# All 64 second-layer scatters in one row in the attention stage, two in flight

## What is computed

```
xn = layernorm(x)
x  = x + attention(xn) + moe(xn)
```

```
h = rmsnorm(xn) * norm_w                    # 2048 x 256
top 4 of 32 experts by softmax(h @ gate_w.T), weights renormalised
pos = rank of a token within its expert; those past the capacity are dropped
buf[expert, pos] = h[token]                 # the scatter
eo = (silu(buf @ w13_gate) * (buf @ w13_up)) @ w2
out[token] += weight * eo[expert, pos]
```

## Time and profile before

| what | value |
|---|---|
| median of three runs | 1323.95 us |
| the profiled execution, its own time | 1324.33 us |
| its span | 1323.1 us |
| TensorE busy | 1102.8 us (83%) |
| DVE busy | 780.4 us (59%) |
| ACT busy | 522.8 us (40%) |
| POOL busy | 510.3 us (39%), 487 instructions |
| mean granted TensorE clock | 0.921 |
| second route stage | from 890.9 us to the barrier ahead of 957.06 us |
| attention stage | from 957.06 us to the barrier ahead of 1069.65 us |

### The profile page before, as it was taken

One profiled execution on the slowest core, in us unless ns is written; L12 is line 12 of the kernel. 1 busy time (PEld: TensorE's weight loads), 2 busy tenths in 40 slices (PEclk: granted clock), 3 DMA queues, 4 the chain that ended last, 5 costly groups with the idle time before them and its releaser, 6 DMA issues. The chain is left out here.

```text
span 1323.1 us, 19843 instructions
## 1 busy us (share of the span) xinstructions
PE 1102.8 (83%) x5538; PEld 827.4 (63%) x5538; DVE 780.4 (59%) x1925; ACT 522.8 (40%) x1419; POOL 510.3 (39%) x487
## 2 busy tenths in 40 slices
PE   5659999999969999688889999959679979999100
PEld 5436667777859998355557777855357658888100
DVE  5868776666115554599997776257337545545233
ACT  2336765555204444355555555031123324444000
POOL 0657776565000000565565564033634300000575
PEclk9879999999979999699999999979969979999655
DMA  9432222221455654422222221035579235554343
GB/s 359 186 100 84 89 93 80 76 72 53 191 143 175 182 180 156 109 75 76 77 72 72 77 72 32 1 84 230 184 223 273 101 93 163 162 162 156 99 130 112
DMA packets 116998, 167.21 MB, mean 126 GB/s; under 512 B 15248, under 2 KB 88848, under 8 KB 114832
## 3 DMA queue, kind: packets, MB, share of 16 engines
q1 hardware_dynamic: 77248, 107.46, 26.3%
q0 software_dynamic: 12288, 33.57, 8.0%
q10 hardware_dynamic: 27360, 24.92, 5.4%
HBM read 103.11 MB, written 62.78 MB: 125 GB/s over the span
## 5 line engine op out<-in xcount | busy, mean ns | idle before, releaser
L1219 PE MATMUL bank<-big_a,probsT 128*128 x760 | 201.8, 361 | 0.1
L856 POOL TENSOR_TENSOR parts<-wq,parts 128x256 fp32r<-128x256 f32 x64 | 48.9, 764 | 382.6 <-ACT parts L1101 382.6
L1110 ACT ACTIVATE probs<-bank,negmax 128x256 f32<-128x256 f32 (+3 forms) x256 | 135.0, 537 | 121.4 <-DVE negmax L1025 112.8
L917 PE MATMUL bank<-kT,qT 128*128 128x256 f32 (+3 forms) x512 | 171.7, 457 | 0.0
L933 PE MATMUL bank<-const,probs 128*128 128x128 f32 x640 | 129.6, 275 | 26.8 <-DVE probs L1037 26.7
L949 PE MATMUL bank<-probsT,big_b 128*128 128x512 f32 (+3 forms) x512 | 149.1, 434 | 0.0
L1219 PEld LDWEIGHTS bank<-big_a,probsT 128*128 128x128 f32 x760 | 131.6, 196 | 20.8 <-issue 2.2
L1025 DVE TENSOR_REDUCE negmax<-bank 128x1 f32<-128x256 f32 (+3 forms) x256 | 113.6, 486 | 47.4 <-PE bank L919 46.2
L1297 DVE TENSOR_TENSOR work<-work,bank 128x96 f32<-128x96 f32 (+1 forms) x190 | 51.6, 271 | 151.5 <-ACT work L1264 151.4
L1708 POOL DMA_INDIRECT big_a<-ys_dram,slot_r x64 | 62.4, 975 | 200.2 <-PEq L1691 181.0
L901 PE MATMUL bank<-parts 128*128 128x512 f32 x256 | 116.9, 492 | 20.3 <-POOL parts L856 15.3
(11 more groups left out here) (210 smaller groups left out, 2023.3 us busy)
## 6 DMA issues: line engine op xcount, KB each, us to landing
probs<-xs_dram SPq DMA_DIRECT2D x190, 128.0 KB
ys_dram<-work ACTq DMA_DIRECT2D x190, 128.0 KB
work<-khT_dram SPq DMA_DIRECT2D x64, 256.0 KB
xs_dram<-big_a SPq DMA_DIRECT2D x12, 1024.0 KB, 20.0
wq<-in_wq SPq DMA_DIRECT2D x64, 128.0 KB
big_a<-in_gu SPq DMA_DIRECT2D x1, 6144.0 KB, 18.2
stack_dram<-parts SPq DMA_DIRECT2D x24, 256.0 KB
xlow<-stack_dram SPq DMA_DIRECT2D x48, 128.0 KB
```

Of the source, the lines that this page charges most:

```text
L917: nc.tensor.matmul(s.ps[bank][:, at:at + w], s.qT[:, par, i * P:(i + 1) * P], s.kT[:, par, 0:w], start=True, stop=False)
L1110: nc.scalar.activation(s.probs[:, par, ROW_AT[i]:ROW_AT[i] + (i + 1) * P], s.ps[bank][:, at:at + (i + 1) * P], ACT.Exp, bias=s.negmax[:, p ...
L1219: mm = nc.tensor.matmul(s.ps[2 + i % 2][:, 0:W], rowsT[:, i % 2, k * P:(k + 1) * P], gu[:, k, bass.ds(e * W, W)], start=k == 0, stop=k == ...
```

## The change

The 24 scatters of the second route stage are taken out of it, with the wait for the slots and the wait for their landing. All 64 scatters are issued by POOL in the attention stage, in one row, tile by tile and choice by choice. They wait no longer for `shift_ready` of any unit. In front of scatter n (from the third on) POOL waits until scatter n - 2 has landed. At the end it waits for all 64.

```
--- before.py
+++ after.py
@@ -34,7 +34,6 @@
 USED_TILES = (TOKENS * TOPK + EXPERTS * (P - 1)) // P
 UNROLL = 4
 STEPS = 8
-EARLY_TILES = 6
 CAP1 = 2 * TOKENS * TOPK // EXPERTS
 OUT_OF_RANGE = 1 << 16
 
@@ -472,13 +471,8 @@
                     nc.gpsimd.tensor_tensor(k_lo, k_full, k_hi.bitcast(F32), ALU.subtract).then_inc(low_ready, 1)
 
                 split_low(0)
-                pool.wait_ge(slots_done, 1)
                 for b in range(1, BATCH):
-                    for t in (2 * b - 2, 2 * b - 1):
-                        scatter_tile(nc, s, d, 1, t, moved)
                     split_low(b)
-                for k in range(TOPK):
-                    pool.wait_ge(moved[k], 16 * EARLY_TILES)
 
         @block.scalar
         def _(act):
@@ -1512,13 +1506,14 @@
 
         @block.gpsimd
         def _(pool):
-            late = [(t, k) for t in range(EARLY_TILES, TILES) for k in range(TOPK)]
-            for u in range(NU):
-                pool.wait_ge(shift_ready, u + 1)
-                for t, k in late[len(late) * u // NU:len(late) * (u + 1) // NU]:
+            for t in range(TILES):
+                for k in range(TOPK):
+                    n = t * TOPK + k - 2
+                    if n >= 0:
+                        pool.wait_ge(moved[n % TOPK], 16 * (n // TOPK + 1))
                     scatter_tile(nc, s, d, 1, t, moved, (k,))
             for k in range(TOPK):
-                pool.wait_ge(moved[k], 16 * (TILES - EARLY_TILES))
+                pool.wait_ge(moved[k], 16 * TILES)
 
         @block.tensor
         def _(pe):
```

## The result

| | before | changed |
|---|---|---|
| median of 4 runs each | 1323.53 us | 1345.60 us |
| ratio | | 1.0167 (95% interval 1.0149 to 1.0185) |
| the profiled execution, its own time | 1324.33 us | 1344.64 us |
| its span | 1323.1 us | 1342.9 us |

The change costs 22 us. That it would cost time was forecast, how much was not: 1331.5 us was forecast, 7.6 us more than before, and 1345.6 lies outside the range of 1318.3 to 1341.

The account below looks back on a forecast made before the run. POOL's scatters were taken to bound the route stage's end, TensorE the attention stage. With the new row ending after TensorE, the expert stage starts 7.6 us later: 1324.33 + 7.6 = 1331.9, median 0.38 lower, 1331.5 us; range 1318.3 to 1341.

Parts of the forecast that it names:

- The route stage (6.1 us earlier): End of second route stage: without 24 scatters POOL's low parts end sooner, stage ends 6.1 us earlier, bounds 5.5 and 6.7.
- The first loads (1.0 us): Attention stage's start: some 5 scatters beside SP's first loads delay TensorE by 1.0 us, bounds 0 and 1.8.
- The stage ends with the last landing, and SP starts 0.82 us later: Attention stage's end: last scatter lands at 1076.5, SP starts the expert stage 0.82 us after, at 1077.3.
- nothing else of POOL is queued behind the waits: Attention stage's end: POOL has no further work of its own after its waits; no time was added for any.
- The row's length: Attention stage: 64 scatters paced by landing plus restart over two, last landing 12.8 us after TensorE's part ends.
- The free spacing (1.59): Row on nearly free DMA engines: (2.4 landing + 0.78 restart) / 2 = 1.59 us per scatter.
- the full stretch: Row from 966 to 1004 us, DMA engines loaded: landing 4.5 us, spacing 2.64, 14.4 scatters.
- the half-full stretch: Row from 1004 to 1024 us, DMA share 0.78: landing 3.4 us, spacing 2.1, 9.5 scatters.
- 5 to 7 us: Landing times read from two loaded scatters in the earlier trace, behind others in flight and expert weights.
- The clock (0, bound +4): Expert stage's start: TensorE, idle longer before it, may start at the lower clock; taken as 0, bounds 0 and +4 us.
- The first (the row is hidden): Attention stage: landings stay near 2.4 us, row lands at 1054, TensorE's end decides, 1318.9 us; chance 0.22.
- the third rival: Attention stage: SP's queue starves the row, landings 6.0 and 4.5 us, row 17 us late, 1341 us; chance 0.12.

Follow-up runs that it names:

- experiments 1 and 2: 1: changed kernel without the wait on scatter n - 2, 1317.03 us; 2: changed route stage, four attention-stage scatters behind each unit's shift_ready, 1320.15 us.
- experiment 3: Changed kernel, but SP loads the attention stage's expert weights only after all 64 scatters landed: 1327.61 us, with a shorter layer 0 in it.
- experiment 4: Changed kernel, but each scatter waits for the one just before it, one in flight: 1413.58 us, with a shorter layer 0 in it.

## Why the prediction was right and wrong

**The route stage (6.1 us earlier): right.** Measured 6.6 us. The mechanism holds, POOL's scatters between ACT and the last low part, and experiments 1 and 2 get the same 59.6 to 59.7 us.

**The first loads (1.0 us): too much, within its bounds.** TensorE's first matmul (timeline of PE) comes 9.5 us after SP's first load at 952.37, against 9.4 before, although four scatters start beside the loads:

```profile
961.89 0.80 PE L1536 MATMUL bank<-xlow 96*128 96x512 f32 x1 [11.48 <-DMA probs<-in_sums]
```

DVE ends at 1063.98, or 1062.1 without the 1.9 us ahead of the stages; 1063.7 was forecast.

**"The stage ends with the last landing, and SP starts 0.82 us later": this step failed.** The prediction took the 0.82 us from DVE's end and gave it to POOL's. Behind POOL's last landing come a DRAIN of 5.28 us and the barrier, 6.3 us. Half of the attention stage's miss is this term, and by itself it is more than the 4.6 us by which the time lies above the range. It stood in the trace of before, as a DRAIN of 3316 ns, hidden; "nothing else of POOL is queued behind the waits" was wrong.

**The row's length: the mechanism right, the term under-sized by 5.4 us.** The free spacing (1.59) is as measured. In the full stretch the landing was taken as 4.5 us and is 4.2 in the median; 15 scatters start there and 14.4 were forecast. The misses are beside it: 4 and not 5.4 in the first loads, 8 and not 9.5 in the half-full stretch, where the landing is 4.1 in the median and not 3.4. With 30 scatters by then in place of 32.5, 2.5 more go at 1.59 each, 4 us; the rest is a few single late steps, such as 1.56 us of idle time at 1042.78 among those of 0.92. That the landing in the full stretch came out as forecast is in part luck: "5 to 7 us" reads too much into the earlier trace rows, where the scatter of 978.84 has its packets between 983 and 985, which is 4 to 6 us.

**The clock (0, bound +4): about right.** The expert stage takes 164.5 in place of 163.6 us. The granted clock is 0.59 in 1090 to 1100 and 1.00 from 1100 on (changed, the last two rows); in the same first 10 us of the stage it was 0.70 before (first row):

```profile
1070.00:1080.00 10.00, 8.31 (x34) 6.11 (x35) 3.11 (x10) 2.37 (x6) 0.00 (x0) 0.70 0.40 118
...
1090.00:1100.00 10.00, 8.25 (x29) 6.06 (x30) 2.92 (x10) 2.05 (x5) 0.00 (x0) 0.59 0.34 105
1100.00:1200.00 100.00, 100.00 (x556) 84.48 (x555) 50.15 (x184) 40.50 (x124) 0.00 (x0) 1.00 0.52 163
```

So the stage began in part at the lower level before as well. The difference of 0.9 us is within the bounds; that it is the clock's was not tested.

**The rivals.** The first (the row is hidden) falls with its constant landing: the landings go with the load, 4.2 us in the median of one stretch and 2.4 in another. The Trainium skill, DMA: Bandwidth & Descriptors, anatomy of one DMA by the GpSimd path, gives a fit by which 128 KB take 2.3 us, an estimate from its figures. The trace agrees on free DMA engines (2.4 us) and not under load (4.2). That the landings are in part a matter of what SP has queued is shown by experiment 3; that the engines' turns between queues are the way in which it comes about is not shown by any run. What the third rival priced, 1341 us, was nearer in time than the forecast, but not by its mechanism: landings of 6.0 us did not occur in the median. What made up the difference was the DRAIN, in no case of mine. The range was too short at the top because it priced only terms of the row.

What beats both kernels most is the changed one without its wait (experiment 1), or with four in flight: 1318.19 us (1317.86 to 1318.62) against 1324.48.

## What to carry to other kernels

A bound on DMAs in flight turns a row of issues into a row of landings: its spacing is (landing + restart of the issuing engine) / number in flight, and never less than the spacing without a bound (1.28 us here). The landing has to be taken under the load that the row will meet, and with the number in flight. Multiply by the count and compare with the end of the work that covers it, before counting what was saved elsewhere.

When work is moved so that another engine closes a stage, look at what that engine does between its last wait and the barrier. These are queue instructions that no busy time counts, and while they are hidden their length looks harmless.

## What the runs showed that I had not expected

POOL's DRAIN takes 82 ns for each indirect DMA of 128 rows since its last DRAIN, also for those landed long ago, and some 40 to 55 ns besides (64: 5280 ns; 40: 3316, which is 82 ns less for each of the 24; 2: 207; 1 behind a hidden one: 136). It does not end before the DMAs in flight have landed.

In the attention stage three in flight are 23.6 us better than two, and four only 1.0 us better than three: the gain ends where the row with its DRAIN gets inside TensorE's work.

The attention of batches 2 and 3 in layer 0 takes 327 us in most profiles and 305 in two, with kernels that do not differ there. DVE is what differs: between 600 and 700 us it is busy for 96.6 us with 161 instructions in the trace of before and for 85.3 us with 184 in that of experiment 4, and its additions of 128 x 256 values to x take 1087 ns in the mean in the one and 479 ns in the other. What makes the two is not shown.
